# Gated cross-attention block with routed experts: the heads' sums by way of DRAM, divided eight heads at a time

## What is computed

```python
x = x + tanh(g_xattn) * xattn(layernorm(x), ctx)
x = x + tanh(g_ffn) * ffn(layernorm(x))

def xattn(x, c):
    y = softmax(causal(q @ k.T * scale)) @ v          # own sequence
    y = y + softmax(qc @ kc.T * scale) @ vc           # context
    return y.heads_to_channels() @ Wp + bp

def ffn(x):
    out = expert(x, sg, su, sd)                       # shared
    for e in range(7): out += w[..., e:e+1] * expert(x, rg[e], ru[e], rd[e])
    return out                                        # w: top 2 of softmax(x @ wr.T + rb)
```

## Time and profile before

| | |
|---|---|
| median of 3 runs | 1414.56 us |
| the profiled execution | 1413.27 us |
| its span | 1411.5 us |
| PE busy | 1368.6 us (97%) |
| DVE busy | 880.9 us (62%) |
| ACT busy | 727.3 us (52%) |
| POOL busy | 365.4 us (26%) |
| granted TensorE clock, mean | 0.993 |

### The profile page before, as it was taken

How to read it: one execution, slowest core, us unless ns; L and a number is a source line. 1 busy time by engine, 2 the same in 40 slices (tenths; PEclk the granted TensorE clock), 3 DMA queues, 4 the chain that set the end, 5 groups by cost and what they waited for, 6 DMA issues and landing times.

```text
span 1411.5 us, 27301 instructions
## 1 busy us (share of the span) xinstructions
PE 1368.6 (97%) x7688; PEld 694.0 (49%) x7689; DVE 880.9 (62%) x1804; ACT 727.3 (52%) x1107; POOL 365.4 (26%) x743
## 2 busy tenths in 40 slices
PE   7988999999999999999999999989999999999997
PEld 4544333333333333333333333364556777777775
DVE  6776888888888888888888888653532222222221
ACT  4644667677777676767676767732210222222221
POOL 5655222222222222222222222200001232233232
PEclk9999999999999999999999999999999999999999
DMA  8754111111111111111111111057004122112111
GB/s 246 237 186 154 43 53 51 48 50 48 47 49 50 51 50 50 49 48 48 48 51 51 50 49 50 7 218 297 0 1 134 26 33 34 30 30 37 30 30 23
DMA packets 57711, 98.43 MB, mean 70 GB/s; under 512 B 7441, under 2 KB 42001, under 8 KB 56657
## 3 DMA queue, kind: packets, MB, share of 16 engines
q1 hardware_dynamic: 50384, 88.10, 18.8%
q0 software_dynamic: 7296, 9.97, 4.5%
HBM read 69.20 MB, written 28.58 MB: 69 GB/s over the span
## 4 chain that ended last, share of the span: by engine, by line
PE 88%; DMA 2%; DVE 2%; ACT 1%; issue 1%; POOL 1%; SPq 0%; POOLq 0%; ACTq 0%; DVEq 0%
PE ps L669 19%; PE ps L834 13%; PE ps L651 13%; PE ps L551 13%; PE ps L847 7%; PE ps L786 5%; PE ps L797 3%; PE ps L718 3%; PE ps L654 2%; PE ps L565 2%; PE ps L858 2%; DMA k_parts<-work 2%; PE ps L555 1%; PE ps L592 1%; PE ps L625 1%
## 5 line engine op out<-in xcount | busy, mean ns | idle before, releaser
L1242 DVE TENSOR_REDUCE mx<-ps 128x1 f32<-128x512 f32 (+1 forms) x832 | 515.1, 662 | 99.6 <-PE ps L551 69.3
L993 ACT ACTIVATE arena<-ps 128x1024 f32<-128x1024 f32 (+1 forms) x512 | 484.3, 995 | 138.7 <-PE ps L651 135.2
L669 PE MATMUL ps<-arena 128*32 128x512 f32 (+5 forms) x2432 | 290.9, 525 | 0.6 <-ACT arena L993 0.4
L551 PE MATMUL ps<-arena 96*128 96x512 bf16 x768 | 263.0, 382 | 7.3 <-DMA arena<-k_parts 2.9
L651 PE MATMUL ps<-arena 98*128 98x512 bf16 x832 | 264.4, 381 | 5.0 <-DMA arena<-rowst 4.9
L1144 POOL TENSOR_SCALAR_AFFINE_SELECT arena<-arena 128x128 f32<-128x128 f32 x256 | 74.8, 292 | 439.2 <-ACT arena L993 429.3
L834 PE MATMUL ps<-arena,work 128*128 x608 | 186.4, 460 | 0.6 <-issue 0.6
L551 PEld LDWEIGHTS ps<-arena 96*128 96x128 bf16 x768 | 74.1, 96 | 178.0 <-DVE mx L1242 103.2
L1520 DVE TENSOR_TENSOR work<-work,ps 128x352 f32<-128x352 f32 x76 | 39.6, 521 | 179.1 <-ACT work L1061 179.1
L834 PEld LDWEIGHTS ps<-arena,work 128*128 128x128 f32 x608 | 112.5, 190 | 57.4 <-issue 1.1
L1242 DVE TENSOR_REDUCE mneg<-ps 128x2 f32<-128x512 f32 (+2 forms) x192 | 112.4, 640 | 23.9 <-PE ps L561 23.4
(11 more groups left out here) (161 smaller groups left out, 1406.8 us busy)
## 6 DMA issues: line engine op xcount, KB each, us to landing
arena<-in_experts SPq DMA_DIRECT2D x8, 2176.0 KB, 12.2
arena<-k_parts SPq DMA_DIRECT2D x64, 198.1 KB
arena<-k_parts SPq DMA_DIRECT2D x64, 132.1 KB
arena<-q_parts SPq DMA_DIRECT2D x64, 96.0 KB
k_parts<-work SPq DMA_DIRECT2D x16, 300.0 KB, 5.2
q_parts<-work SPq DMA_DIRECT2D x12, 384.0 KB, 5.4
arena<-k_parts SPq DMA_DIRECT2D x64, 66.0 KB
arena<-q_parts SPq DMA_DIRECT2D x64, 64.0 KB
```

The source lines that it names most:

```text
L551: mm = pe.matmul(out, qx[:, qt * P:(qt + 1) * P], ks[0:KROWS, T + j * CHUNK:T + (j + 1) * CHUNK], start=True, stop=True)
L669: mm = pe.matmul(ps[32 * q:32 * q + VW, 6, b0:b1], vst[0:kn, r % VR, TT + kt if cross else kt, :], pr[0:kn, c0:c0 + b1 - b0], start=(phase ...
L993: act.activation(pr[:, c0:c0 + n], ps[:, 2 * (g % 2):2 * (g % 2) + 2, :].rearrange("p b n -> p (b n)")[:, 0:n], ACT.Exp, scale=SCALE).then ...
L1242: return dve.tensor_reduce(m, out, AX_X, ALU.max)
```

## The change

- `norm`, `norm_out`, `cross_sums`, `head_output`, DVE's `reciprocals`, the 32 transposes of y and ACT's eight copies of them are gone. `norm` in the ring becomes `spare`: nothing runs there, and `bank_free` looks three entries further back when it meets it.
- ACT still copies bank 6 to `osb`. SP now stores `osb` (128x512) to a DRAM tensor `o_parts` in each step, and ACT's next copy waits for that store.
- After each eighth head SP loads eight tiles of 128x512 from `o_parts`: three context denominators and the own one (each row read 16 times, with a source of 8 heads by 16 repeats by 512), and three context numerators and the own one (8 heads by 16 rows by 512). The rows are then channels, already in the layout of `xnT`.
- In the step after, POOL adds the denominators (two adds of 128x512, ahead of mask 1) and the numerators (two adds, ahead of masks 2 and 3). DVE takes the reciprocals of both 128x512 tiles, after its pieces 12 and 14. POOL multiplies twice and adds.
- The hardware loop has 7 turns of eight steps, and six steps stand behind it. Seven groups are done in its eighth steps, the last one in the tail.
- The first head's row of maxima is loaded as soon as it is there, five stores earlier in SP's queue.
- In the tail, sequences 0 to 2 are projected, then `turn_xn(0)` and three of six pieces of `shared_up(0)` come, then the projection of sequence 3. DVE takes the last group's reciprocals ahead of the first three pieces of `shared_hidden(0)`. The shared expert's weights are loaded from ACT's queue.

```diff
+    with eng.Fori(0, TURNS) as i:
+        for h in range(GH):
+            step(i * GH + (h + 2), (h + 2) % NR, True, True, True, i if h == GH - 1 else None)
...
+            def sums_store(v):
+                sp.wait_ge(S["o_evac"], v + 1)
+                sp.dma_start(o_parts[bass.ds(v, 1)].rearrange("a p t -> (a p) t"), osb).then_inc(S["o_written"], 16)
+            def parts_load(j):
+                sp.wait_ge(S["parts_free"], j + 1)
+                sp.wait_ge(S["o_written"], j * (16 * GH) + 16 * GH)
+                heads = o_parts[bass.ds(j * GH, GH)]
+                for q, dst in enumerate([*cross_den, self_den]):
+                    src = heads[:, VW * q + D:VW * q + D + 1, :].to_broadcast([GH, D, T])
+                    sp.dma_start(dst, src).then_inc(S["parts_in"], 16)
+                for q, dst in enumerate([yT[:, bass.ds(j, 1), :].rearrange("p a t -> p (a t)"), *cross_num, self_num]):
+                    sp.dma_start(dst, heads[:, VW * q:VW * q + D, :]).then_inc(S["parts_in"], 16)
+            with sp.Fori(0, TURNS) as i:
+                for h in range(GH):
+                    r = h % NR
+                    sp.wait_ge(S["qk_done"], i * (GH * NG) + NG * (h + 1))
+                    stack_loads(i * GH + (NR + h), r)
+                    sums_store(i * GH + h)
+                    rows_load(i * GH + (h + 2), (r + 2) % NR)
+                    if h == GH - 1:
+                        parts_load(i)
...
+            def den_sums(j):
+                pool.wait_ge(S["parts_in"], j * 128 + 128)
+                pool.tensor_tensor(cross_den[0], cross_den[0], cross_den[1], ALU.add).then_inc(S["den_half"], 1)
+                pool.wait_ge(S["den_half"], j + 1)
+                pool.tensor_tensor(cross_den[0], cross_den[0], cross_den[2], ALU.add).then_inc(S["den_sum"], 1)
...
+                if group is not None:
+                    den_sums(group)
                 mask(u, 1, 2)
+                if group is not None:
+                    num_sums(group)
                 mask(u, 2, TT)
+                if group is not None:
+                    outputs(group)
...
+            def cross_reciprocals(j):
+                dve.wait_ge(S["den_sum"], j + 1)
+                dve.reciprocal(cross_den[0], cross_den[0]).then_inc(S["cross_recip"], 1)
+            def self_reciprocals(j):
+                dve.wait_ge(S["parts_in"], j * 128 + 128)
+                dve.reciprocal(self_den, self_den).then_inc(S["self_recip"], 1)
...
+            for b in range(B - 1):
                 project(b)
+            turn_xn(0)
             pe.wait_ge(S["shared_load"], 16)
-            shared_up(0)
+            shared_up(0, 0, SPLIT_UP)
+            project(B - 1)
+            shared_up(0, SPLIT_UP, IT)
```

More of the change, by code:

```diff
@@ L108, in schedule @@
         if g == 3:
-            out += [("values", 0), ("norm",)]
+            out += [("values", 0), ("spare",)]
         if g == 5:
@@ L117 @@
 PE_ORDER = schedule()
-ENTRIES = [item for item in PE_ORDER if item[0] in ("max", "norm", "rows")]
+ENTRIES = [item for item in PE_ORDER if item[0] in ("max", "spare", "rows")]
 RING = 3
@@ L131, in run_steps @@
     step(1, 1, True, True, True)
[L132 to L137, removed]
+    with eng.Fori(0, TURNS) as i:
+        for h in range(GH):
+            step(i * GH + (h + 2), (h + 2) % NR, True, True, True, i if h == GH - 1 else None)
+    for u in range(GH * TURNS + 2, NU):
         step(u, u % NR, True, u + 1 < NU, u + 2 < NU)
@@ L419, in program @@
         SETUP = turn_end[1]
+        ROWS_LOAD_AT = 1 + min(s for n, s in split_of.items() if n >= ROWS_AT)
         BIAS_AT = []
@@ L577, in bank_free @@
                         pe.wait_ge(S["max_red"], min(n, NU * NMAX - MAXED) if isinstance(n, int) else n)
-                elif before[0] == "norm" and not (isinstance(u, int) and u == 0):
-                    pe.wait_ge(S["norm_evac"], step)
                 elif before[0] == "rows":
@@ L709, in step @@
                     pe.wait_ge(S["pool_chain"], 3 * NR + 3)
-            def norm(u):
-                if isinstance(u, int) and u > 1:
-                    pe.wait_ge(S["norm_evac"], u - 1)
-                pe.wait_ge(S["o_evac"], u)
-                out = bank_of("norm")
-                for t in range(TT):
-                    mm = pe.transpose(out[:, t * P:(t + 1) * P], osb[:, t * P:(t + 1) * P], ident[:, :])
-                mm.then_inc(S["norm_mm"], 1)
             pe.wait_ge(S["prep_freed"], len(pieces))
@@ L1318, in _, with step @@
                                       ALU.add).then_inc(S["prep_freed"], 1)
-            def reciprocals(u):
-                dve.wait_ge(S["sums_in"], u)
-                if not (isinstance(u, int) and u == 1):
-                    dve.wait_ge(S["y_parts"], u - 1)
-                dve.reciprocal(rsum[:, :, :], sums[:, :, 2:4, D]).then_inc(S["rsum_ready"], 1)
-            def step(u, r, prev, nxt, nxt2):
+            def cross_reciprocals(j):
[4 more added lines that the diff above has]
+                dve.reciprocal(self_den, self_den).then_inc(S["self_recip"], 1)
+            def step(u, r, prev, nxt, nxt2, group=None):
                 for c in range(NMAX):
@@ L1378, in tail_scale, with residual @@
                 scale_rows(t)
-            for t in range(NT):
+            def residual(t):
                 dve.wait_ge(S["proj_mm"], t + 1)
@@ L1383, in _ @@
                                          op0=ALU.mult, op1=ALU.add).then_inc(S["x2_ready"], 1)
+            early = NT - TT
+            for t in range(early):
+                residual(t)
                 if t >= 1:
```

183 lines of the change are left out of this document (94 added, 89 removed).

## The result

The changed kernel takes 1524.66 us (median of 4 runs, 1523.47 to 1525.61), the kernel before 1414.89 us beside it (4 runs): ratio 1.0776, 95% interval 1.0757 to 1.0794. It is 110 us slower. The profiled execution has a span of 1521.7 us at a mean granted clock of 0.952.

What follows compares the result with a forecast made beforehand. PE, busy 97% of the span, was taken as the bound. 1413.3 - 18.9 (transposes) + 92.4 (seven groups) + 17.5 (clock) - 5 (start) + 2 (tail) = 1501.3, median 1502 us; own range 1480 to 1525, overall 1444 to 1528.

Steps and rivals of the forecast that it cites:

- The transposes: PE's four transposes of the sums removed from each of 63 steps: gain 0.30 us a step, -18.9 us in all.
- The store: SP's store of the sums in each step: hidden in SP's idle time, cost 0, at most 16 us.
- The eight loads: A group's loads, carried by 8 engines, land late for mask 1: PE waits 5.7 us a group.
- rival of sixteen engines: A group's loads spread over 16 engines, so no wait at mask 1: 1446 to 1453 us, chance 0.11.
- The reciprocals: DVE's two 128x512 reciprocals a group, 4.0 us each, stop PE twice: 7.5 us of waits a group.
- rival of a cheap reciprocal: DVE inverts 512 elements at the rate of a maximum, almost hidden: 1453 us, chance 0.04.
- What it should look like: Signs in the profile after: steps of 12.0 us, each eighth about 27, two 4.0 us reciprocals, DMA shares at most 0.5.
- POOL's other operations: POOL's other five operations of a group, 5.2 us, stand behind masks 1, 2 and 3: counted as 0.
- The clock: After a group's long waits PE runs at half speed: 2.5 us a group, +17.5 in all (0 to 35).
- The start: Earlier first row of maxima shortens PE's wait where the heads begin: -5 us (bounds -3.6 and -7).
- The tail: Behind the last group, reciprocals delay shared_up(0), which ends near 968 instead of 967: +2 us (-4 to +8).
- rival of a doubled body: Longer loop body costs code fetches at each turn, or rows of maxima come late: 1517 to 1530 us, chance 0.10.

Runs made afterwards that it cites:

- e_none: Changed kernel without the seven in-loop groups' loads, adds, reciprocals and products (outputs of 56 heads left out): 1394.15 us, ratio 0.9859 to the kernel before.
- e_16: Changed kernel with the sums laid out in DRAM so each of a group's eight loads reads one contiguous block: 1481.5 us, ratio 1.0485 to the kernel before.
- e_copy: Changed kernel with both 128x512 reciprocals of a group replaced by same-shape copies, output left undivided: 1478.5 us, ratio 1.0466 to the kernel before.
- e_start: Kernel before with only the first load of the row of maxima issued earlier, right after that row is written: 1409.16 us, ratio 0.9971.
- e_tail: Changed kernel with xn's first rows stored before the first expert's weights are loaded in the tail: 1521.14 us, ratio 1.0764 to the kernel before.
- v_spread: v_compact with its transfers spread over steps, at most two loads behind each row of maxima, one whole group per loop turn: 1400.23 us, ratio 0.9916.
- v_compact: Changed kernel with denominators loaded once, one 128x64 reciprocal broadcast through DRAM, POOL's work behind mask 3, and the tail's stores reordered: 1438.79 us, ratio 1.0185.
- e_late16: e_late with the contiguous DRAM layout of e_16 for the group's eight loads: 1509.59 us, ratio 1.0695 to the kernel before.
- e_late: Changed kernel with POOL's adds moved behind mask 3 and both reciprocals one step later: 1542.09 us, ratio 1.0917 to the kernel before.

## Why the prediction was right, and where its terms were off

The sum was 1502 us and the measurement 1524.7, inside the case's own range of 1480 to 1525 by 0.3 us. All of its mechanisms were there: eight engines, mask 1, two stops behind reciprocals, the clock. That the time still fell in that range is in part luck, since two errors of about 25 us cancel. The terms:

- *The transposes*, -0.30 a step: measured -0.38 (12.28 to 11.91, 55 steps), above the 0.32 us that I took as a ceiling. Where the other 0.06 us come from has not been looked into.
- *The store*, 0: right, by `e_none`.
- *The eight loads*, wait of 5.7: measured 9.5 (10.46 in the group shown). Two steps failed. "From 603.38 + 0.68" had SP go straight on, but SP waits for the last store, which lands after 7.3 us: 3.0 us instead of 0.7. And 13.7 us from first issue to landing were 15.9; the next head's stacks and its store run beside the last of the loads (share 0.76 from 484 to 486), but what the 2.2 us are has not been shown. The engine count was right: shares of 0.46 to 0.50, and by `e_16` 16 engines cut the wait by 5.8 us, where I had said 5.7. I had said that the wait would then be 0, and it stayed 3.7: in a group of `e_16` the loads begin 3.4 us after the row and not 0.7, and take 9.2 us and not 7.4. So the rival of sixteen engines was priced too low as well (1446 to 1453, for 1481 measured). The Trainium skill's rule that an outermost dimension below 16 confines a DMA to at most that many engines (DMA: Bandwidth & Descriptors, "Rules for kernel authors") agrees with these shares.
- *The reciprocals*, 4.0 us each and 7.5 us of waits: 3.34 us and 4.1 to 4.8 us of waits. The slope of 7.5 ns from 4 to 16 elements was too steep for 512; 3340 / 512 is 6.5 ns. PE also came later to the first stop, since it ran at half clock. Taking them out gained 47.5 us in the seven steps, near the 7 x 7.5 = 52 of the prediction, but only 28.8 of it was waiting for DVE. The rival of a cheap reciprocal was priced too low (1453, where `e_copy` measured 1478.5 with copies).
- *What it should look like*: ordinary steps of 11.9 (12.0 forecast), an eighth of 30.6 in the mean (27).
- *POOL's other operations*, 0: right, though each took 1.26 us, not 1.04: PE waits for POOL only at mask 1. The 1.04 us of the earlier trace rows were a mean over shapes, of which 128x512 takes 1.14 to 1.16 us.
- *The clock*, 2.5 a group: 18.7 - 9.5 - 4.1 leaves 5.1 us. How much of it is clock has not been shown, but the windows from 490 to 494 and from 502 to 508 run at 0.50 and 0.52, 9 to 10 us in which PE works at half speed. I had given the second stop a "may".
- *The start*, -5: -3.0 in the trace, which is less than the bound of -3.6, and -4.2 by `e_start`. ACT's table load and its wait stood behind the row.
- *The tail*, +2 (-4 to +8): +7.0. Late next was the store of xn's first rows, which I had not looked at; without it the reciprocals are (`e_tail`), and without the reciprocals the store still is (`e_copy`).

So the mask wait was short by 3.8 x 7 = 27 us, the clock by 2.6 x 7 = 18, the tail by 5 and the start by 2; the waits behind the reciprocals were 3.4 x 7 = 24 too large, and the steps gained 5 more. That is 23 us, and the span came out 1521.7 - 1499.5 = 22 us over its forecast. The rival of a doubled body had a chance of 0.10 and gave 1517 to 1530; the time fell there, but its mechanisms added nothing to it: `e_none` has the same body, and the row cost 0.4 us.

## What to carry to other kernels

A long wait covers everything that becomes late during it; before moving work off its path, list what else was issued late in its shadow. Here the row of maxima took the wait over in full (10.9 us for 9.5). Bytes of low urgency are best put into a shared queue a piece per step, behind the small urgent transfer, and not a megabyte at once. In `v_spread` this took v_compact's 1439 us to 1400. And do an elementwise operation with a high price per element before the broadcast, not after it.

## What the runs showed of the hardware that was not expected

- SP needs 0.6 to 0.8 us to issue a load of 256 KB whose source has three dimensions and 0.33 to 0.49 us for a contiguous one (eight: 6.6 us, and 4.0 in `e_late16`).
- A 4 KB load, whose packets run 1.3 us after its issue in the kernel before, came 11 us after it in `e_late`, although the 2 MB ahead of it in its queue had landed 8 us earlier. From 492 to 496, while it was waited for, the share was 0.19, three engines of 16. With the 2 MB in another queue it took 8.9 us.
- A reciprocal of 128x512 takes 3.34 us, a copy of the same shape 0.55 to 0.63 us (`e_copy`), and an add on POOL 1.26 us.
- With copies in place of reciprocals the mask wait stayed at 9.5 us and yet 47.5 us went from seven steps, more than the 28.8 us that PE had waited for DVE. In the changed kernel PE works at 0.50 to 0.52 for 9 to 10 us a group, after its two stops, and in `e_copy` for about 6, after one.
